# The second attention of a three-layer block: float16 pairs, a ring of three banks and a table of ring items

## The reference

```python
x = x + _L0_attn_a_ref(_layernorm(x, axis=-1), ...)   # 16 heads of 64, no mask
x = x + _L0_ffn_ref(_layernorm(x, axis=-1), L0_ffn_W1, L0_ffn_b1, L0_ffn_W2, L0_ffn_b2)
x = x + _L0_attn_b_ref(_layernorm(x, axis=-1), ...)   # 8 heads of 128, causal, rotary
x = x + _L0_ffn_ref(_layernorm(x, axis=-1), L0_ffn_W1, L0_ffn_b1, L0_ffn_W2, L0_ffn_b2)
```

```python
q = _rope(jnp.einsum('btm,mhd->bthd', x, w_aq))
k = _rope(jnp.einsum('btm,mhd->bthd', x, w_ak))
v = jnp.einsum('btm,mhd->bthd', x, w_av)
s = jnp.einsum('bihd,bjhd->bhij', q, k) / D_HEAD
s = s - jnp.asarray(INF_APPROX, x.dtype) * mask      # mask: i < j
o = jnp.einsum('bhij,bjhd->bihd', jax.nn.softmax(s, axis=-1), v)
r = jnp.einsum('bihd,hdm->bim', o, w_ao)
```

## Time and profile before

| what | value |
|---|---|
| median of 3 runs | 2078.3 us (2077.17 to 2080.09) |
| the profiled execution | 2082.57 us |
| its span | 2080.7 us |
| mean granted clock of PE | 0.976 of full speed |
| PE, PEld, DVE, ACT, POOL busy | 94%, 69%, 72%, 71%, 61% |
| first score matmul of the second attention | 1322.8 us |
| its last value matmuls end | 2034.2 us |

### The profile page before, as it was taken

The page is one execution under the profiler, slowest core; times in us unless marked ns, Lnnn a source line. Parts: engine busy times, 40 slices in busy tenths (PEclk is TensorE's granted clock), DMA queues, the critical chain, the costliest instruction groups (busy, mean ns, idle before and its releaser), DMA issues.

```text
span 2080.7 us, 51602 instructions
## 1 busy us (share of the span) xinstructions
PE 1965.4 (94%) x21751; PEld 1435.1 (69%) x21751; DVE 1507.5 (72%) x2818; ACT 1481.2 (71%) x1812; POOL 1279.6 (61%) x687
## 2 busy tenths in 40 slices
PE   4999999999999999999999967899999999999997
PEld 3466666666666666666666544678888787888885
DVE  7888888788888888888888756566676666667642
ACT  2798998998989988999989852355545455554563
POOL 4899999998999999999999852131312223131200
PEclk8999999999999999999999988899999999999999
DMA  5100110110011001101100010000000000000000
GB/s 137 32 20 15 32 32 10 25 32 21 18 28 32 17 17 33 25 17 25 32 17 17 2 52 1 0 1 1 1 1 1 1 1 1 1 1 1 1 1 21
DMA packets 45013, 37.67 MB, mean 18 GB/s; under 512 B 8304, under 2 KB 44144, under 8 KB 44528
## 3 DMA queue, kind: packets, MB, share of 16 engines
q1 hardware_dynamic: 43824, 33.60, 6.6%
q10 hardware_dynamic: 960, 0.79, 0.2%
HBM read 8.15 MB, written 1.05 MB: 4 GB/s over the span
## 4 chain that ended last, share of the span: by engine, by line
PE 86%; DVE 8%; POOL 2%; issue 2%; ACT 1%; ACTq 0%; DMA 0%; POOLq 0%; DVEq 0%
PE ST L1354 10%; PE ST L1355 10%; PE OO L1491 8%; PE RING L1229 7%; PE OO L1298 6%; PE OO L1300 6%; PE OO L1297 6%; PE OO L1229 3%; PE RING L1444 3%; PE ST L1514 3%; PE ST L1491 3%; PE ST L1518 3%; PE RING L1424 3%; PE ST L1516 3%; POOL PAB L517 2%
## 5 line engine op out<-in xcount | busy, mean ns | idle before, releaser
L517 POOL TENSOR_TENSOR PAB<-PR,PAB 128x1024 f16<-128x1024 f32 x342 | 723.7, 2131 | 62.3 <-ACT PAB L655 62.3
L655 ACT ACTIVATE PAB<-ST,exp_scale 128x1024 f16<-128x1024 f32 x512 | 567.0, 1107 | 0.0
L903 DVE TENSOR_REDUCE maxes<-RING 128x1 f32<-128x512 f32 x679 | 450.9, 685 | 132.8 <-PE RING L1229 131.5
L1297 PE MATMUL OO<-VP,PAB 128*128 128x66 f16 x4096 | 446.9, 193 | 2.4 <-POOL PAB L517 2.4
L1298 PE MATMUL OO<-VP,PAB 128*128 128x64 f16 x4096 | 447.5, 194 | 0.0
L1300 PE MATMUL OO<-VP,PAB 128*128 128x66 f16 x4096 | 445.5, 192 | 0.0
L653 ACT ACTIVATE PR<-ST,exp_scale 128x1024 f32<-128x1024 f32 x342 | 381.2, 1115 | 85.7 <-PE ST L1355 83.1
L1297 PEld LDWEIGHTS OO<-VP,PAB 128*128 128x128 f16 x4096 | 380.5, 96 | 78.0 <-issue 15.8
L1298 PEld LDWEIGHTS OO<-VP,PAB 128*128 128x128 f16 x4096 | 377.3, 97 | 61.3
L1354 PE MATMUL ST<-QL,KH 128*128 128x512 f16 x1024 | 388.8, 380 | 2.1 <-ACT PAB L655 1.2
L1355 PE MATMUL ST<-QH,KL 128*128 128x512 f16 x1024 | 389.0, 380 | 0.0
(11 more groups left out here) (202 smaller groups left out, 3260.0 us busy)
## 6 DMA issues: line engine op xcount, KB each, us to landing
KH<-HS SPq DMA_DIRECT2D x120, 64.0 KB, 2.0
QL<-HS SPq DMA_DIRECT2D x64, 64.0 KB, 2.0
QL<-LS SPq DMA_DIRECT2D x64, 64.0 KB, 2.0
QH<-HS SPq DMA_DIRECT2D x64, 64.0 KB, 2.0
KL<-LS SPq DMA_DIRECT2D x60, 64.0 KB, 2.0
X<-in_L_attn_a_x SPq DMA_DIRECT2D x4, 256.0 KB, 3.9
SHARED<-in_rope_cos SPq DMA_DIRECT2D x1, 1024.0 KB, 4.9
SHARED<-in_rope_sin SPq DMA_DIRECT2D x1, 1024.0 KB, 7.9
```

Of the source, the lines that this page charges most:

```text
L517: pool.tensor_tensor(PB[:, s, :], PRA[g % PR_SLOTS], PA[:, s, :], ALU.subtract).then_inc(p_low_ready, 1)
L655: act.activation(PA[:, step % SLOTS_A, :], ST[step % 2][:, :], ACT.Exp, scale=scale).then_inc(sa.exps, 1)
L903: dve.reduce_max(maxes[:, i // BLOCKS, i % BLOCKS:i % BLOCKS + 1], bank[:, :], X_AXIS).then_inc(sa.ring_taken, 1)
L1297: pe.matmul(o, high, v[:, 0:V2_AT], start=(m == 0 and qt == 0), stop=False, skip_group_check=True)
```

## The change

- All operands of the second attention become pairs of float16. Weights are scaled by a power of two for each head and split in twelve pieces during heads 2 to 4 of the first attention, two POOL instructions and one ACT copy for each piece (L600, L606, L725 of the new kernel). The layer norm's transpose is split too (ACT copies, DVE subtracts). A projection is three float16 matmuls.
- A score tile is written by PE alone. Its first matmul multiplies four rows of masked row maxima (`MROW`) with a constant (`row_units`); three key-query products follow. `fill`, "spread" and their copies go.
- ACT takes the exponential twice, in float32 (L785) and in float16 (L787). POOL subtracts (L643). Three value matmuls of 130, 128 and 130 columns replace the float32 one, and they run two steps behind the scores (`LAG_B`), waiting for POOL.
- The fourth query tile of every unit lies in `QUARTER[2]`. The bank that this frees is the third one of the ring (`RING3B`), and `claim` looks three items back. DVE takes the fourth tile first and signals it (`fourth_taken`).
- `PLAN_B` lists the ring items of a head step by step, one string for each step: a digit is one maximum of that unit, r its rows, P, V, T and O a projection, values, turned and output. Digits below a unit's own number stand for the next head.

```diff
+V1B_AT = 2
+V2B_AT = V1B_AT + DB
+VB = V2B_AT + DB
...
+PLAN_B = [
+    ["2 2", "2", "2 T", "P O"],
+    ["2 V", "2", "2 V", "2 2 2", "2 2", "T", "r2 3 P", "O"],
...
+        PRB = [PR[:, 0, 0:BLK], PR[:, 0, BLK:2 * BLK], PBUF[:, 4 * BLK:5 * BLK]]
+        PAH = PBUF[:, 0:2 * BLK].bitcast(F16).rearrange("p (s q) -> p s q", s=SLOTS_B)
+        PAL = PBUF[:, 2 * BLK:4 * BLK].bitcast(F16).rearrange("p (s q) -> p s q", s=SLOTS_B)
...
-        OB = [(O[0], QUARTER[2]), (O[1], QUARTER[3])]
+        OB = [(O[0], QUARTER[2]), (O[1], QUARTER[2])]
+        RING3B = [RING[0], RING[1], QUARTER[3]]
...
+                i = u - UNITS_A
+                if 0 <= i < PIECES_B and step == 0:
+                    pool.wait_ge(b_scaled, 1)
+                    wait(pool, wb_high, i - 1)
+                    pool.tensor_tensor(wb_tmp[:, i % 2, :, :],
+                                       RAW[:, i * 2 * DB:(i + 1) * 2 * DB].rearrange("p (a c) -> p a c", c=DB),
+                                       b_up[:, 2 * i:2 * i + 2].unsqueeze(2).broadcast_to((P, 2, DB)), ALU.mult
+                                       ).then_inc(wb_put, 1)
+                if 0 <= i < PIECES_B and step == 4:
+                    pool.wait_ge(wb_high, i + 1)
+                    pool.tensor_tensor(piece_b(WLB, i), wb_tmp[:, i % 2, :, :], piece_b(WHB, i), ALU.subtract
+                                       ).then_inc(wb_low, 1)
...
+            for g, (it, ul, step) in enumerate(PLACES_B):
+                c0 = max(0, step - BT * (ul % BLOCKS)) * P
+                pool.wait_ge(sbb.exps, g + 1)
+                wait(pool, sbb.pv, g - SLOTS_B + 1)
+                pool.tensor_tensor(PAL[:, g % SLOTS_B, c0:BLK], PRB[g % PR_SLOTS_B][:, c0:BLK],
+                                   PAH[:, g % SLOTS_B, c0:BLK], ALU.subtract).then_inc(p_low_ready_b, 1)
+                for head, n, j in projects_before(g, 1):
+                    rope_sum_b(j, n)
+                for head, n, j in projects_before(g, 4):
+                    low_b((head + 1) % 2, j, (head + 1) * 2 * BLOCKS + j)
...
+                i = u - UNITS_A
+                if 0 <= i < PIECES_B and step == 2:
+                    act.wait_ge(wb_put, i + 1)
+                    act.activation(piece_b(WHB, i), wb_tmp[:, i % 2, :, :], ACT.Copy).then_inc(wb_high, 1)
...
+            def values_high_b(hs, part, bank, item):
+
+                act.wait_ge(sbb.ring_put, item + 1)
+                act.activation(VBS[:, hs, part * BT:(part + 1) * BT, V1B_AT:V2B_AT],
+                               bank[:, :].rearrange("p (t c) -> p t c", c=DB), ACT.Copy).then_inc(vb_high, 1)
...
+                scale = exp_scale_b[:, head:head + 1]
+                wait(act, p_low_ready_b, g - PR_SLOTS_B + 1)
+                act.wait_ge(sbb.scores, g + 1)
+                act.activation(PRB[g % PR_SLOTS_B][:, c0:BLK], SB[g % 2][:, c0:BLK], ACT.Exp, scale=scale)
+                wait(act, sbb.pv, g - SLOTS_B + 1)
+                act.activation(PAH[:, g % SLOTS_B, c0:BLK], SB[g % 2][:, c0:BLK], ACT.Exp, scale=scale
+                               ).then_inc(sbb.exps, 1)
...
-                    link(dve.tensor_copy(negparts[:, 0:BT].bitcast(F32R), negmax[:, :]))
-                    dve.tensor_tensor(negparts[:, BT:AUX], negmax[:, :], negparts[:, 0:BT],
-                                      ALU.subtract).then_inc(s.max_ready, 1)
+                    dve.tensor_scalar(negparts[:, :], negmax[:, :], 1.0 / ROW_UNIT, lifts_b[:, head:head + 1],
+                                      ALU.mult, ALU.add).then_inc(s.max_ready, 1)
...
-                o = three[:, 0:3 * VB].rearrange("p (a c) -> p a c", c=VB)
-                dve.reciprocal(rden[:, 0:3], o[:, :, DB])
-                link(dve.reciprocal(rden[:, 3:4], fourth[:, DB:VB]))
-                dve.tensor_tensor(AB[:, 0:3, :], o[:, :, 0:DB], rden[:, 0:3].unsqueeze(2).broadcast_to((P, 3, DB)),
-                                  ALU.mult)
-                dve.tensor_scalar(AB[:, 3, :], fourth[:, 0:DB], rden[:, 3:4], None, ALU.mult
+                o = three[:, 0:3 * V2B_AT].rearrange("p (a c) -> p a c", c=V2B_AT)
+                dve.reciprocal(rden[:, 0:3], o[:, :, 0])
+                link(dve.reciprocal(rden[:, 3:4], fourth[:, 0:1]))
+                dve.tensor_scalar(AB[:, 3, :], fourth[:, V1B_AT:V2B_AT], rden[:, 3:4], None, ALU.mult
+                                  ).then_inc(sbb.fourth_taken, 1)
+                dve.tensor_tensor(AB[:, 0:3, :], o[:, :, V1B_AT:V2B_AT],
+                                  rden[:, 0:3].unsqueeze(2).broadcast_to((P, 3, DB)), ALU.mult
                                   ).then_inc(sbb.o_taken, 1)
...
             def claim(s, item):
 
-                wait(pe, s.ring_taken, item - 1)
+                wait(pe, s.ring_taken, item - 2)
...
-                pe.wait_ge(sbb.wst_ready, head + 1)
-                blk = j // 2
-                pe.matmul(bank[:, :], WST[:, hs, (j % 2) * DB:(j % 2 + 1) * DB], XNT[:, blk * BLK:(blk + 1) * BLK],
-                          start=True, stop=True).then_inc(sbb.ring_put, 1)
-
-            def values_b(hs, part, bank, item, head):
+                pe.wait_ge(wb_low, PIECES_B)
+                q = slice(j // 2 * BLK, (j // 2 + 1) * BLK)
+                w = slice(j % 2 * DB, (j % 2 + 1) * DB)
+                pe.matmul(bank[:, :], WHB[:, head, w], XH[:, q], start=True, stop=False)
+                pe.matmul(bank[:, :], WLB[:, head, w], XH[:, q], start=False, stop=False)
+                pe.matmul(bank[:, :], WHB[:, head, w], XL[:, q], start=False, stop=True).then_inc(sbb.ring_put, 1)
...
                 at = qb * BLK + i * P
                 if c == qb:
-                    pe.matmul(bank[:, i * P:(i + 1) * P], ident_r[:, :], later_keys[:, :], start=True, stop=True)
-                pe.matmul(bank[:, 0:width], QH[hs][:, at:at + P], KH[hs][:, c * BLK:c * BLK + width],
+                    pe.matmul(bank[:, i * P:(i + 1) * P], mask_ident[:, :], later_keys[:, :], start=True, stop=True)
+                pe.matmul(bank[:, 0:width], QH16[hs][:, at:at + P], KH16[hs][:, c * BLK:c * BLK + width],
                           start=(c < qb), stop=True, skip_group_check=True).then_inc(sbb.ring_put, 1)
...
+                keys = slice(step * P, (step + 1) * P)
+                c0 = max(0, step - BT * qb) * P
+                q = slice(qb * BLK + c0, (qb + 1) * BLK)
+                tile = SB[g % 2][:, c0:BLK]
+                pe.matmul(tile, row_units[:, :], MROW[:, qb % 2, c0:BLK], start=True, stop=False,
+                          skip_group_check=True)
+                if step >= BT * qb:
+                    pe.matmul(SB[g % 2][:, c0:c0 + P], mask_ident[:, :], later_keys_t[:, :], start=False,
+                              stop=False, skip_group_check=True)
+                pe.matmul(tile, KH16[hs][:, keys], QH16[hs][:, q], start=False, stop=False, skip_group_check=True)
+                pe.matmul(tile, KL16[hs][:, keys], QH16[hs][:, q], start=False, stop=False, skip_group_check=True)
+                pe.matmul(tile, KH16[hs][:, keys], QL16[hs][:, q], start=False, stop=True, skip_group_check=True
+                          ).then_inc(sbb.scores, 1)
...
-                    pe.wait_ge(sbb.exps, g + 1)
+                    if step == 0:
+                        pe.wait_ge(sbb.ring_taken, VALUES_OF_B[it * 2 + hs] + 1)
+                        wait(pe, sbb.o_taken, it * UNITS_B + ul - 1)
+                    pe.wait_ge(p_low_ready_b, g + 1)
+                v = VBS[:, hs, step, :]
                 for qt in range(max(2 * half, step - BT * qb), 2 * half + 2):
-                    bank, at = (OB[ul % 2][0], qt * VB) if qt < 3 else (OB[ul % 2][1], 0)
-                    ins = pe.matmul(bank[:, at:at + VB], PRB[:, step % 2, qt * P:(qt + 1) * P],
-                                    VBS[:, ul // BLOCKS, step, :], start=(step == 0 and qt in (0, 3)),
-                                    stop=(step == BT * qb + qt), skip_group_check=True)
+                    if step == 0 and qt == 3:
+                        wait(pe, sbb.fourth_taken, it * UNITS_B + ul)
+                    bank, at = (OB[ul % 2][0], qt * V2B_AT) if qt < 3 else (OB[ul % 2][1], 0)
+                    o = bank[:, at:at + V2B_AT]
+                    tile = slice(qt * P, (qt + 1) * P)
+                    high, low = PAH[:, g % SLOTS_B, tile], PAL[:, g % SLOTS_B, tile]
+                    pe.matmul(o, high, v[:, 0:V2B_AT], start=(step == 0 and qt in (0, 3)), stop=False,
+                              skip_group_check=True)
+                    pe.matmul(o[:, V1B_AT:V2B_AT], high, v[:, V2B_AT:VB], start=False, stop=False,
+                              skip_group_check=True)
+                    ins = pe.matmul(o, low, v[:, 0:V2B_AT], start=False, stop=(step == BT * qb + qt),
+                                    skip_group_check=True)
                 if half == 1:
                     ins.then_inc(sbb.pv, 1)
...
+                elif g > 1:
+                    scores_b(g)
```

(28 more changed lines are left out.)

581 lines of the change are left out of this document (281 added, 300 removed), and 2 rows, old and new, of the table PLAN_B.

## The result

The changed kernel takes **2063.19 us** (median of 4 runs, 2062.52 to 2065.53), the kernel before 2078.27 (2077.17 to 2080.09). The ratio is 0.9928, with an interval of 0.9916 to 0.9940: 15 us faster, under 1%, but clear of the noise. Forecast were 2000 us, so 63 of the 78 us of gain did not come. In the profiled executions the span went from 2080.7 to 2063.7 us.

A forecast was written before the change was run, and what follows sets the result against it. PE, busy 94% of the span, was taken as the bound. Second attention -84 us (work -65, waits -19), first attention +5, between 0, end +1: -78, so 2004.6 profiled and 2000 us as median; range 1968 to 2045.

The forecast's parts named there:

- signs of being wrong: Value matmuls over 0.065 us apart, second-attention waits over 60 or under 25 us, or first attention longer by over 13.
- Scores: four matmuls x 0.215 = 0.86: Second attention, each full step: the row-maximum matmul and three score products at 0.215 us each, 0.86 where 0.69 stood.
- Value products at 0.057, plain steps of 1.54: Second attention: float16 value matmuls 0.057 us apart, 0.68 for four tiles; a full step 1.54 us instead of 1.58.
- load-paced value products: Rival, second attention: weight loads pace value matmuls at 0.096 us each, +127 us, 2127 in all; chance 0.03.
- a spacing of 0.081: Rival, second attention: value load and matmul pairs 0.081 us apart, +79 us, 2079 in all; chance 0.02.
- Waits, 59 to 40: Second attention: PE's waits fall from 59 to 40 us, 19 less; called the least certain term.
- Work of 587 us: Second attention: PE's added-up matmul work without waits, 587 us after the change against 652 before, 65 less.
- The lumps: Rival, second attention: the chain through POOL and DVE's queue costs 85 us of waits, not 40; 2045 us; chance 0.22.
- First attention: ... I take 5: First attention: 24 added POOL instructions, 13 us of work, lengthen it by 5 us, between 0.3 and 13.
- Start, 0: Kernel start, up to the first negated maxima: no change forecast, 0 us.
- Between the attentions, -4 to +4: From the first attention to the first score matmul of the second: +3, +1 and -4 us, net 0.
- End, +1: Kernel end: values two steps behind with a narrow POOL step add 1 us.

## Why the prediction was wrong

The faster side was right; the size was not, and 2063 lies outside the range of 1968 to 2045. Even the side was luck: with the 40 us of waits that it allows for, the 64 and the 19 us that it did not have would have made the kernel some 5 us slower, and only the waits, some 20 lower than forecast, brought it out ahead. Two of its signs of being wrong came true (waits under 25 us, a first attention longer by over 13), and the mechanism behind most of the miss was in none of its rivals. By its own steps:

- **"Scores: four matmuls x 0.215 = 0.86"** is the step that failed. The row-maximum matmul was priced like its neighbours because it has as many columns and the same type. It costs 0.32, and 0.10 more in front of it: 0.2 x 320 = 64 us. With 128 rows the term holds: 0.22 each, and a step of 1.55. The kernel before had one with 8 rows, L1473, and its timeline shows the same thing (the prediction priced it at 0.23): 512 columns, 0.43 to the next start where 0.23 is the rule, and 0.27 in front of it where the 384 columns of L1518 take 0.18 elsewhere.

```profile
1434.71 0.34 PE L1518 MATMUL ST<-QL,KH 128*128 128x384 f32 x1
1434.98 0.50 PE L1473 MATMUL RING<-MROW,ones_r 8*128 8x512 f32 x1
1435.41 0.71 PE L1491 MATMUL OO<-PAB,PR 128*128 128x129 f32 x4
```

- **Value products at 0.057, plain steps of 1.54**: right (0.057; 1.55 with 128 rows). The rivals of load-paced value products and of a spacing of 0.081 are refuted. Yet the idea behind them, a weight load that shows, came true at another matmul. The Trainium skill, "TensorE: Matmul & The Clock Gate", section "The mechanism", says that a weight load overlaps running matmuls only if it goes to other rows of the array, or to the background buffer. The trace agrees with the buffer for 128 rows after 128 (0.057, although a load's record is 0.097). That a load of 4, 32 or 64 rows loses the overlap on both sides is shown by these runs; why it does is open.
- **Waits, 59 to 40**: too high. Work of 587 us and a stage of 607 (128 rows) leave 20; in the changed kernel 587 + 64 of 670 leave 19. Both are what is left beside an added-up sum, not a measured wait. Of the 40 that went, the third bank carries 22. What the table and the dropped `filled` wait gave of the rest was not separated. The lumps did not come.
- **"First attention: ... I take 5"**: it was +24.3. The part that the step meant, POOL's time, is 8.3, inside its 0.3 to 13. The other 16 are a mechanism that the prediction did not have: the lock between DVE and POOL, with the low clock behind each hole. The sign was in the trace of before: the same line took 5.31 us once, where 0.23 is the rule.
- **Start, 0**: +3.0 in the profile. In eleven traces of the changed kernel and its variants that leave this stage alone, the first negated maxima come between 56.7 and 62.0, mostly under 60, so this is hardly the change's. **Between the attentions, -4 to +4**: -4.6. **End, +1**: +2.0.

In one sum: -78 forecast, +64 for the row-maximum matmul, -22 for waits and small terms of that stage (what is left of its -41.7), +19 for the first attention, +3, -5 and +1 for the rest, which is -18, for a span that shrank by 17.0.

On the lock: the Trainium skill, "SBUF — State Buffer", section "Who interferes with whom", says that VectorE and GpSimd share a pair of ports under an exclusive lock. VectorE asks for it in two-port forms (which use this pair beside its own) such as tensor_scalar, except the form that writes out its accumulator, and with two inputs in SBUF. Every run here agrees: tensor_scalar and scalar_tensor_tensor were held up, the accumulator form never. That the thing held is a pair of ports no trace shows; which forms are held up, they do. By that rule an instruction waits out the other's one instruction; here it waited out two to four in a row. What lets it through nearly always (60 of 64 times it took 1.03 us at most, once 1.65) and three times not was not found. Nor is the number fixed: the run with 32 rows had a fourth such instruction, of 5.02 us.

## What to carry to other kernels

Price each matmul by its rows as well as its columns and type. Where a few rows are added between full float16 matmuls, pad the operands to 128 rows with zeros, which saved 61 us here. When GpSimd runs back to back, look at the longest time, not only the median, of each short VectorE instruction that someone waits for: here one rewritten instruction was worth 26 us. Count with a hole also the low clock behind it. Before moving work onto a busy GpSimd or ScalarE, ask who shares its ports, and what 0.08 us more does to an engine with a tenth of air.

## What was not expected of the hardware

- A float16 matmul with 4, 32 or 64 operand rows between matmuls of 128 rows takes 0.10 us more on each side (0.32 and 0.15 instead of 0.215 and 0.057); with 128 rows nothing.
- A VectorE instruction on 128x4 numbers was held up by GpSimd for 7.04 us, over four of its instructions; its accumulator form took 0.216 to 0.220 us at every one of 64 times.
- A scalar_tensor_tensor of that size was held up the same way (7.036 us).
- Behind holes of 6.15, 6.14 and 4.42 us PE resumed at a granted clock of 0.50, for 3.9, 5.1 and 4.6 us.
- A bias vector in an exponential on 128x1024 lengthens the distance from 1.01 to 1.09 us.
